# A two-layer convolution block on one core: POOL forms part of the bilinear shift, DVE and PE share the rest anew

## The reference, cut to what matters

```python
x = x + L0(_gn(x))     # layer 0: bilinear shift by channel, then a 1x1 convolution
x = x + L1(_gn(x))     # layer 1: Haar transform, conv, depthwise conv, two 1x1 convs, conv, inverse Haar

# layer 0: each channel is shifted by its own (dy, dx) with |dy|, |dx| < 1
s = z1 * (1 - dy) * (1 - dx) + z2 * (1 - dy) * dx + z3 * dy * (1 - dx) + z4 * dy * dx
s = s * w_dw[None, :, None, None]
return jnp.einsum('bchw,oc->bohw', s, w_pw)
```

## Time and profile before

| what | us |
|---|---|
| median of 3 runs | 5330.59 (5328.4 to 5332.22) |
| the profiled execution | 5333.35 |
| its span, first to last instruction | 5331.7 |
| PE busy | 4655.7 (87%) |
| DVE busy | 4621.4 (87%) |
| ACT busy | 4330.6 (81%) |
| POOL busy | 1158.6 (22%) |
| mean granted TensorE clock | 0.963 |

### The profile page before, as it was taken

How to read it: one execution, slowest core, us unless ns; L and a number is a source line. 1 busy time by engine, 2 the same in 40 slices (tenths; PEclk the granted TensorE clock), 3 DMA queues, 4 the chain that set the end, 5 groups by cost and what they waited for, 6 DMA issues and landing times. The chain is left out here.

```text
span 5331.7 us, 54963 instructions
## 1 busy us (share of the span) xinstructions
PE 4655.7 (87%) x12634; PEld 2160.9 (41%) x12634; DVE 4621.4 (87%) x4447; ACT 4330.6 (81%) x6469; POOL 1158.6 (22%) x853
## 2 busy tenths in 40 slices
PE   2889999999999999999999999999987777777775
PEld 1334434344343443444434666666642222222222
DVE  8989899998999989999808999999468888888887
ACT  5888888888888888888837888888578888888887
POOL 0000000000000000000006888888211111111111
PEclk7999999999999999999999999999999999999998
DMA  8989999999999999999972333333159999999999
GB/s 344 364 338 374 427 396 422 426 394 427 389 425 426 394 427 392 427 391 346 361 280 96 133 135 132 133 135 135 44 120 225 236 236 236 236 236 236 236 236 223
DMA packets 248867, 1542.06 MB, mean 289 GB/s; under 512 B 29424, under 2 KB 29808, under 8 KB 91504
## 3 DMA queue, kind: packets, MB, share of 16 engines
q1 hardware_dynamic: 156528, 936.14, 44.7%
q0 software_dynamic: 36864, 268.45, 24.3%
q10 hardware_dynamic: 55296, 335.57, 15.2%
HBM read 877.35 MB, written 662.70 MB: 289 GB/s over the span
## 5 line engine op out<-in xcount | busy, mean ns | idle before, releaser
L1175 PE MATMUL ps<-arena,c2T 128*128 128x512 f32 x2048 | 1025.1, 652 | 366.3 <-ACT arena L919 363.7
L997 PE MATMUL ps<-arena 128*128 128x512 f32 x2048 | 968.3, 617 | 19.6 <-DVE small L1340 17.2
L976 PE MATMUL ps<-arena 128*128 128x512 f32 x2048 | 964.9, 598 | 7.7 <-DVE arena L1407 6.5
L972 PE MATMUL ps<-arena 128*128 128x512 f32 x1536 | 743.7, 607 | 105.7 <-ACT ps L625 49.2
L1175 PEld LDWEIGHTS ps<-arena,c2T 128*128 128x128 f32 x2048 | 401.9, 205 | 988.8 <-ACT arena L919 558.7
L919 ACT ACTIVATE arena<-ps,small 128x512 f32<-128x512 f32 x1024 | 713.0, 778 | 98.5 <-DVE arena L1618 90.4
L1502 DVE SCALAR_TENSOR_TENSOR ps<-arena,taps,ps 128x1024 f32<-128x1024 f32 (+1 forms) x602 | 655.5, 1132 | 15.6 <-PE ps L1122 13.7
L625 ACT ACTIVATE ps<-arena 128x1024 f32<-128x1024 f32 x512 | 526.4, 1028 | 161.8 <-ACT arena L666 149.1
L544 POOL TENSOR_SCALAR arena<-arena 128x256 f32<-128x256 f32 x112 | 114.7, 1029 | 2484.6 <-DMA arena<-in_x 2440.1
L666 ACT ACTIVATE arena<-ps,small 128x1024 f32<-128x1024 f32 x512 | 564.3, 1102 | 86.3 <-PE ps L976 85.7
L997 PEld LDWEIGHTS ps<-arena 128*128 128x128 f32 x2048 | 385.9, 189 | 546.1 <-issue 539.9
(11 more groups left out here) (169 smaller groups left out, 6010.4 us busy)
## 6 DMA issues: line engine op xcount, KB each, us to landing
arena<-in_x SPq DMA_DIRECT2D x508, 1024.0 KB, 12.8
out_x<-arena ACTq DMA_DIRECT2D x256, 1024.0 KB, 8.8
out_x<-arena POOLq DMA_DIRECT2D x256, 1024.0 KB, 17.0
arena<-out_x SPq DMA_DIRECT2D x208, 1024.0 KB, 15.0
y_dram<-arena ACTq DMA_DIRECT2D x128, 512.0 KB, 8.3
arena<-y_dram SPq DMA_DIRECT2D x128, 512.0 KB, 3.4
h_dram<-arena SPq DMA_DIRECT2D x112, 512.0 KB, 2.6
arena<-h_dram SPq DMA_DIRECT2D x112, 512.0 KB, 10.2
```

The source lines that it names most:

```text
L972: mm(ps[:, r, :], w_right[:, :], cells(r, 1), start=False, stop=False, skip_group_check=True)
L976: last = mm(ps[:, r, :], w_center[:, :], cells(r, 0), start=False, stop=True, skip_group_check=True)
L997: last = mm(ps[:, 4 + s % 2, :], w_c1b[:, q, :], cells[:, q // 2, q % 2, :, :], start=(q == 0), stop=(q == 3))
L1175: last = mm(ps[:, 4 * k + q, :], c2T[:, q, :], h2[:, k * HC:(k + 1) * HC], start=True, stop=True)
```

## The change

Four things are changed, all in the first part.

1. In chunks 1, 2 and 3 of each group the up sum is no longer one multiply-add of DVE. POOL forms it in two operations in place: u = up * above, then u = u + x (`add_above`). DVE waits for it ahead of its down sum. POOL waits for slots s-1 and s and for PE to be through with the buffer, and makes the three sums of a group between `copy_top` and `copy_bottom`.
2. DVE adds the right neighbour in chunks 1 and 3 of each group in images 1 to 6, and in chunks 1, 2 and 3 in the last image. PE has correspondingly fewer matmuls.
3. In image 0 PE no longer adds the left neighbour of chunk 1; DVE does. `w_left` and its computation go.
4. The counters of the waits are worked out anew (`v_made`, `left_made`, `above_made`).

```diff
+POOL_CHUNKS = (1, 2, 3)
+RIGHT_DVE = (1, SLOTS - 1)
+RIGHT_DVE_LAST = (1, 2, 3)
...
         def three_in_v(b, s):
 
-            return not (isinstance(b, int) and b == 0) and (s % 2 == 1 if final(b) else s == SLOTS - 1)
+            return not (isinstance(b, int) and b == 0) and s in (RIGHT_DVE_LAST if final(b) else RIGHT_DVE)
...
+            def add_above(b, g, s):
+
+                t = b * NCH + g * SLOTS + s
+                u = u_buf[s][:, :, 1:W + 1]
+                for near in (s - 1, s):
+                    wait_alone(pool, b * (16 * NG) + g * 16 + 16, slot_in[near])
+                wait_alone(pool, nth(t * 2 + 1, 2 * SLOTS), conv_done)
+                pool.tensor_scalar(u, ring[:, s * ROWS:(s + 1) * ROWS, :], up, 0.0, ALU.mult, ALU.add).then_inc(u_above, 1)
+                wait_alone(pool, above_made(b, g, s) - 1, u_above)
+                pool.tensor_tensor(u, u, slot(s), ALU.add).then_inc(u_above, 1)
...
             def image_rows(b):
+                group_rows(b, 0)
                 copy_bottom(b, 0)
                 with pool.Fori(1, NG - 1) as g:
                     copy_top(b, g)
+                    group_rows(b, g)
                     copy_bottom(b, g)
                 copy_top(b, NG - 1)
-
+                group_rows(b, NG - 1)
...
-                    for r in range(2 * half, 2 * half + 2) if left_on_pe(b, s) else ():
-                        mm(ps[:, r, :], w_left, cells(r, -1), start=False, stop=False, skip_group_check=True)
...
-                stt(out=u, in0=ring[:, s * ROWS:(s + 1) * ROWS, :], scalar=up, in1=slot(s),
-                    op0=ALU.mult, op1=ALU.add).then_inc(u_up, 1)
+                if s not in POOL_CHUNKS:
+                    stt(out=u, in0=ring[:, s * ROWS:(s + 1) * ROWS, :], scalar=up, in1=slot(s),
+                        op0=ALU.mult, op1=ALU.add).then_inc(u_up, 1)
...
-                dve.wait_ge(u_up, t + 1)
+                if s in POOL_CHUNKS:
+                    dve.wait_ge(u_above, above_made(b, g, s))
+                else:
+                    dve.wait_ge(u_up, b * NG + g + 1)
```

More of the change, by code:

```diff
@@ L130, in preact_kernel @@
         pwT, w_center, w_right = (cut(P) for _ in range(3))
-        w_left = y1_out[0][:, 0:P]
         c1H, w_c1b = (four(cut(4 * P)) for _ in range(2))
@@ L262, in preact_kernel @@
         consts_made = sem("consts_made")
-        setup_done, w_step = sem("setup_done"), sem("w_step")
+        setup_done = sem("setup_done")
         primed = sem("primed")
@@ L278, in preact_kernel @@
         bias0_ready = sem("bias0_ready")
-        u_up, v_done, v_left = sem("u_up"), sem("v_done"), sem("v_left")
+        u_up, u_above, v_done, v_left = sem("u_up"), sem("u_above"), sem("v_done"), sem("v_left")
         top_copied, bottom_copied = sem("top_copied"), sem("bottom_copied")
@@ L325, in first_pairs, with left_made, above_made @@
             return [divmod(n, SLOTS) for n in (2 * s, 2 * s + 1)]
-        def left_on_pe(b, s):
-            return isinstance(b, int) and b == 0 and s == 1
         def v_made(b, g, s):
-            if isinstance(b, int) and b == 0:
-                return g * (SLOTS - 1) + (1 if s == 0 else s)
-            return b * NCH + g * SLOTS + (s + 1 - NG)
+            return b * NCH + g * SLOTS + (s + 1)
         def three_in_v(b, s):
-            return not (isinstance(b, int) and b == 0) and (s % 2 == 1 if final(b) else s == SLOTS - 1)
+            return not (isinstance(b, int) and b == 0) and s in (RIGHT_DVE_LAST if final(b) else RIGHT_DVE)
+        def left_made(b, g, s):
+            k = len(RIGHT_DVE)
+            if final(b):
+                return g * len(RIGHT_DVE_LAST) + ((B - 2) * NG * k + RIGHT_DVE_LAST.index(s) + 1)
+            return b * (NG * k) + g * k + (RIGHT_DVE.index(s) + 1 - NG * k)
+        def above_made(b, g, s):
+            k = 2 * len(POOL_CHUNKS)
+            return b * (NG * k) + g * k + (2 * POOL_CHUNKS.index(s) + 2)
         def final(b):
@@ L558, in copy_bottom, with group_rows @@
                 copy_row(SLOTS * ROWS + 1, 1).then_inc(bottom_copied, 1)
+            def add_above(b, g, s):
[7 more added lines that the diff above has]
+                pool.tensor_tensor(u, u, slot(s), ALU.add).then_inc(u_above, 1)
+            def group_rows(b, g):
+                for s in POOL_CHUNKS:
+                    add_above(b, g, s)
             def image_rows(b):
+                group_rows(b, 0)
                 copy_bottom(b, 0)
@@ L563, in image_rows @@
                     copy_top(b, g)
+                    group_rows(b, g)
                     copy_bottom(b, g)
                 copy_top(b, NG - 1)
+                group_rows(b, NG - 1)
+            pool.wait_ge(setup_done, 1)
             image_rows(0)
@@ L958, in conv @@
                 k = s % 2
-                near = 1 if left_on_pe(b, s) else 0
                 def cells(r, dx):
-                    return u_buf[s][:, 2 * r:2 * r + 2, near + dx:near + dx + W]
+                    return u_buf[s][:, 2 * r:2 * r + 2, dx:dx + W]
                 for half in range(2):
                     if half == 0:
[L966 to L969, removed]
+                        pe.wait_ge(v_done, v_made(b, g, s))
                     pe.wait_ge(x_in_psum, nth(t * 2 + half))
@@ L1396, in shift_rows @@
                     count_x(*ahead_of, s, range(2, DVE_PIECES))
[L1397 to L1410, removed]
+                dve.wait_ge(u_done, nth(t))
+                v, beside = u_buf[s][:, :, 0:W + 1], u_buf[s][:, :, 1:W + 2]
+                left_added = stt(out=v, in0=v, scalar=left, in1=beside, op0=ALU.mult, op1=ALU.add)
+                if three_in_v(b, s):
+                    left_added.then_inc(v_left, 1)
+                    if ahead_of and not late:
+                        count_x(*ahead_of, s, range(2, DVE_PIECES))
+                    dve.wait_ge(v_left, left_made(b, g, s))
+                    v = u_buf[s][:, :, 0:W]
+                    stt(out=v, in0=u_buf[s][:, :, 1:W + 1], scalar=right, in1=v,
+                        op0=ALU.mult, op1=ALU.add).then_inc(v_done, 1)
+                else:
+                    left_added.then_inc(v_done, 1)
                 if late and not final(b):
@@ L1437, in _ @@
             x_scales(1)
-            ts(tmp, scale0, left, None, ALU.mult).then_inc(w_step, 1)
-            dve.wait_ge(w_step, 1)
-            ts(w_left, pwT[:, :], tmp, None, ALU.mult)
             dve.wait_ge(late_in, 16 * len(LATE_PARAMS))
```

## The result

The changed kernel takes 5795.07 us (median of 4 runs, 5790.56 to 5799.36) beside 5329.49 us for the kernel before: a ratio of 1.087, with a 95% interval of 1.086 to 1.089. It is 466 us slower; the forecast was 5815.

The account below looks back on a forecast made before the run. Bound before: transfers mid-image, engines at an image's start; after: DVE with POOL's turns. Image 0 +68.8, images 1 to 6 +328.3, image 7 +97.4, DVE's last wait -10: +484.5 us, 5815 beside the median; range 5690 to 6060.

Parts of the forecast that it names:

- The bound: First part: DVE with POOL's turns inside it, each group longer than the transfers (40 to 42 us) and PE's 34.4.
- The exclusion: First part: DVE's two-operand multiply-adds and POOL's six new operations a group take turns; 78% with POOL early enough.
- The price, 17.7 us a group: First part: POOL's 19.7 us a group enter DVE's time, less 0.33 us at each of six hand-overs, 2.0 in all.
- What hides, 3.2 us a group: Walking one group with alternating turns: of POOL's time, 3.2 us run beside DVE's counting of x, 6.3 at most.
- The groups: DVE's time for four chunks: 42.0 us in image 0, 46.7 in images 1 to 6, 46.1 in image 7.
- The ends of an image, 10 us: Images 1 to 6: 10 us an image over eight groups, for moments, scales and weights.
- The 30 us kept for the ends of image 0: Image 0: 30 kept of 39.6 us over its groups, for double counting in the first, moments and scales in the last.
- the sum of 484.5: Whole kernel, us: image 0 +68.8, images 1 to 6 +328.3, image 7 +97.4, DVE's wait behind it -10.
- (b): First part: POOL comes late, its list being in order, and DVE waits ahead of down; some 6055 us, 12%.
- (c): First part: PE's gaps lower its clock, 52 us a group, some 6080 us, 5%; sign: granted clock under 0.9.
- (d): First part: long POOL and DVE operations share the access and run side by side, so not slower; 5240 us, 5%.
- The break-even of 10.9 us a group: First part: the change pays only if POOL costs DVE less than 10.9 of its 19.7 us a group.

Follow-up runs that it names:

- sum-only kernel: The changed kernel with POOL's product in chunks 1 to 3 replaced by a fill and its sum kept: 5580.8 us, 1.047 of the kernel before.
- write-only kernel: The changed kernel with POOL's product and sum replaced by three fills of constants for each of its chunks: 5296.99 us, 0.993 of the kernel before.
- the kernel without POOL's sums: The changed kernel with all four up sums back on DVE, the new DVE and PE split kept: 5363.79 us, 1.006 of the kernel before.
- the one with one chunk: The changed kernel with only chunk 2's up sum on POOL and the right sums as before the change: 5402.87 us, 1.013 of the kernel before.
- product only: The changed kernel with POOL's sum in chunks 1 to 3 replaced by a fill and its product kept: 5314.89 us, 0.997 of the kernel before.

## Why the prediction was right, step by step

**The bound.** Right: with the transfers no longer the limit, DVE with POOL's turns inside it sets the pace, 298.86 of 300 us busy. PE's share was forecast at about 70%; it is 82% in that stretch, with a granted clock of 0.94, and the transfers have 374 GB/s for some 355.

**The exclusion.** Right, and now seen from both sides: with the reads 5795 us, with writes in their place 5297 us. The rule of the Trainium skill's "SBUF — State Buffer", section "Who interferes with whom", agrees with the trace in that the two exclude each other. Taken to the letter (nothing saved at a hand-over, 5940 us) it was further off than the price less a hand-over.

**The price, 17.7 us a group.** Measured 3 x 5.4 = 16.2. The hand-over of 0.33 us was nearly right (a sum of 4.16 us costs 3.80, a product of 1.97 costs 1.60; the product was forecast at 2.07), but the sum takes 4.16 us alone, not the 4.49 that I carried on from 1024 and 896 elements: a slope over so short a step, times eight, missed by 0.33.

**What hides, 3.2 us a group.** In the group shown the six operations add 0.45, 3.29, 0.46, 3.80, 1.13 and 4.00 us to the instructions that wait, 13.1 of 16.2, so 3.1 are hidden; over the inner groups the remainder is some 2.6 (32.2 + 16.2 - 45.8), with the row copies in it. The walk with alternating turns held for the first four operations (left 3, right 3, up 0, down 0). The last two came out the other way round: behind left 0 the column copy is not held (0.16 us at 1322.04) and the product has the two counts beside it, while the sum behind down 1 has nothing. The sum of the walk is the same, by luck in these two. In a chunk with a right sum the third count stands between left and right and not ahead of left, as at 1290.98 in the sum-only kernel. The walk did not carry to that kernel.

**The groups.** 46.7 us forecast for images 1 to 6, 43.5 to 47.0 measured away from their ends (mean 45.7, one of 50.8); 42.0 for image 0, 41.8 measured on the mean of its six inner groups (37.3 to 45.4); 46.1 for image 7, 43.5 to 46.8 measured between its ends, which have 50.8.

**The ends of an image, 10 us.** This term was mis-sized. First groups of images 1 to 6 take 51 to 57 us and last groups 54 to 60 (46 in image 6), together some 18 over two inner groups. Before it was some 13.5 where I could have read it: 41.5 for 37.0 in the first group, 45 to 47 for 37 of DVE's own in the last (1.6 of it a wait for x in image 2). The rest fits held small work, such as L1357 at 4378 ns for 480. By down sums, images 1 to 6 take 2299.7 us for a forecast of 2301.6: a group 1.0 us too long, 48 times, against ends 8 us too short, 6 times. The total there is better than its terms: the two errors cancel, by luck.

**The rest.** By up sums, as in the prediction, image 0 took 343.4 us for 366.0, images 1 to 6 2304.9 for 2301.6 and image 7 360.5 for 371.8; DVE's wait behind it fell from 18.85 to 15.37 us, not by 10. The 30 us kept for the ends of image 0 were mis-sized: 343.4 - 8 x 41.8 leaves 9. In all this makes 24 us less than the sum of 484.5.

**The rivals.** (b) POOL late: DVE has no wait for POOL's sums anywhere in the first part, and its idle time there is 26 us. (c) The clock: its sign came, 0.89 on the mean of 100 to 3000, but more work for PE made the kernel faster, and DVE is busy nearly throughout, so the cause isn't there; the sign was ill chosen. (d) Long operations that run side by side: excluded by the multiply-adds of 3.95 and 6.16 us. Its price of 5240 was also too hopeful, since the write-only kernel has 5297: images 1 to 6 stay at 317 to 333 us, not at the 319.2 of a full transfer rate throughout. The break-even of 10.9 us a group was too high. It stands for a group of DVE's own of 41.1 - 1.25 = 39.9 us, but the kernel without POOL's sums (39.4) is 0.6% slower and the one with one chunk (38.9) 1.3% slower; product only (35.4) is 0.3% faster. The groups at an image's start, and images 0 and 7, have no transfer to hide behind, so a mean over groups doesn't decide.

The only versions here that are faster than the kernel before are the write-only and the product-only one, and both leave work out.

## What to carry to other kernels

An idle POOL is no free engine for a DVE that works on two SBUF operands: price each POOL instruction that reads SBUF at its own length less some 0.35 us on DVE's path, unless the counting, or another instruction that the trace shows beside it at its usual length, runs beside it. One operand is no sign of that by itself, as the next section shows. Here 2.37 us of DVE's work was bought with 5.4 us of its waiting, 4.7 after what hides (904 / 192). Before moving work, look in the trace for one short POOL instruction beside a long DVE one and one short DVE instruction beside a long POOL one: their lengths tell the rule, and the waits and idle columns don't. And try the fill in the place of the reading operations: it prices the turns in one run.

## What the runs showed of the hardware that I had not expected

DVE's one-operand copies and products are held as well, and by POOL's writes too (a product on 128 x 128 elements, L1333, has 1.97 us at most in the write-only kernel for 0.28). There the column copy starts with a fill and ends with it (DVE, then POOL; the next copy without a fill takes 0.17 us):

```profile
527.54 1.85 DVE L1389 COPY arena<-arena 128x8 f32<-128x8 f32 x1 [2.02 <-DMA arena<-in_x]
```

```profile
527.55 1.81 POOL L575 MEMSET arena<- 128x2048 f32 x1 [7.03 <-DMA arena<-in_x]
```

So the write-only kernel holds DVE's copies (at most 1853 ns against 421 before) and not its two-operand sums. DVE's counting (`BATCH_NORM_STATS2`) was not held in the changed kernel, 666 to 695 ns in all 768 cases; in the three kernels with fills it is long (up to 1785, 1789 and 1823 ns) in 16, 2 and 7 of 768 cases, every time right behind a held copy, whose end it shares. `TENSOR_REDUCE` (L1345, 208 to 220 ns) was not held in any kernel.

POOL's sum of 2048 elements takes 4157 ns with rows of 258, while 1024 take 2362: less than the slope between 896 and 1024 says.
